# Picked attention of a graph and feed-forward network: two heads' scores laid behind each other in five banks, two banks for turned probabilities, contexts in one piece

## The reference, cut to what matters

```python
q = (normed @ Wq + bq).reshape(b, l, H, dh)      # H = 12 heads of dh = 64
kk = (normed @ Wk + bk).reshape(b, l, H, dh)
v = (normed @ Wv + bv).reshape(b, l, H, dh)
logits = jnp.einsum('blhd,bmhd->bhlm', q, kk) / jnp.sqrt(jnp.float32(dh))
probs = jax.nn.softmax(logits, axis=-1)
ctx = jnp.einsum('bhlm,bmhd->blhd', probs, v).reshape(b, l, d)
attn_out = ctx @ Wo + bo
merged = jnp.where(attn_mask[..., None], attn_out, mix_out)
```

## Time and profile before

| | us |
|---|---|
| median of 3 runs | 2976.41 |
| lowest, highest | 2974.64, 2977.48 |
| the profiled execution's own time | 2970.5 |
| its span | 2968.8 |
| attend_picked in it, first scores to last spread matmul | 2701.4 to 2870.7 |

### The profile page before, as it was taken

The page is one execution under the profiler, slowest core; times in us unless marked ns, Lnnn a source line. Parts: engine busy times, 40 slices in busy tenths (PEclk is TensorE's granted clock), DMA queues, the critical chain, the costliest instruction groups (busy, mean ns, idle before and its releaser), DMA issues. The chain is left out here.

```text
span 2968.8 us, 39008 instructions
## 1 busy us (share of the span) xinstructions
PE 2536.1 (85%) x14382; PEld 2118.7 (71%) x14383; DVE 2106.1 (71%) x3030; ACT 1315.0 (44%) x1649; POOL 310.4 (10%) x166
## 2 busy tenths in 40 slices
PE   6877894888856994799699999699999979998888
PEld 3556892232323994699699999599888769896668
DVE  6775899999974555699689988660567687136555
ACT  1573225989831000222578776221565563222431
POOL 0000000000003794000000000331000000000013
PEclk9997656999976997899899999899999999999989
DMA  2467542611104554455646643452634362311012
GB/s 69 131 174 180 150 150 67 237 52 35 35 33 178 189 197 158 154 180 160 201 121 181 170 118 90 150 171 81 187 122 129 102 194 70 85 54 59 1 41 80
DMA packets 174702, 366.47 MB, mean 123 GB/s; under 512 B 24871, under 2 KB 103541, under 8 KB 174034
## 3 DMA queue, kind: packets, MB, share of 16 engines
q1 hardware_dynamic: 122024, 274.54, 30.9%
q10 hardware_dynamic: 49312, 73.97, 7.4%
q0 software_dynamic: 3200, 15.73, 1.5%
HBM read 281.06 MB, written 83.12 MB: 123 GB/s over the span
## 5 line engine op out<-in xcount | busy, mean ns | idle before, releaser
L1649 PE MATMUL gat_acc<-far_u,gat_ft 125*65 125x512 f32 x720 | 286.3, 538 | 58.1 <-DVE far_u L1717 57.6
L2246 PE MATMUL rg_out<-rg_w,rg_hT 128*125 128x256 f32 (+1 forms) x900 | 276.6, 307 | 8.0 <-POOL rg_w L1185 8.0
L2247 PE MATMUL rg_out<-rg_w,rg_hT 128*125 128x256 f32 (+1 forms) x900 | 275.5, 306 | 0.0
L2248 PE MATMUL rg_out<-rg_w,rg_hT 128*125 128x256 f32 (+1 forms) x900 | 275.3, 306 | 0.0
L1649 PEld LDWEIGHTS gat_acc<-far_u,gat_ft 125*65 125x65 f32 x720 | 93.7, 142 | 246.9 <-issue 153.6
L2246 PE MATMUL rg2a_acc<-rg2a_value_part,rg2a_wts_part 125*125 125x512 f32 x600 | 204.8, 341 | 14.8 <-DVE rg2a_wts_part L1958 11.4
L2247 PE MATMUL rg2a_acc<-rg2a_value_part,rg2a_wts_part 125*125 125x512 f32 x600 | 205.5, 342 | 0.0
L2248 PE MATMUL rg2a_acc<-rg2a_value_part,rg2a_wts_part 125*125 125x512 f32 x600 | 203.8, 340 | 0.0
L1684 ACT ACTIVATE far_u<-gat_rows,gat_ks 125x1250 f32<-125x1250 f32 x118 | 156.7, 1328 | 41.8 <-PE gat_acc L1649 32.7
L2246 PEld LDWEIGHTS rg_out<-rg_w,rg_hT 128*125 128x125 f32 x900 | 169.1, 188 | 8.2 <-issue 8.0
L1697 DVE TENSOR_TENSOR far_u<-far_u,gat_lowb 125x1250 f32<-125x1250 f32 x120 | 174.4, 1454 | 0.4 <-PEq L711 0.4
(11 more groups left out here) (531 smaller groups left out, 6369.3 us busy)
## 6 DMA issues: line engine op xcount, KB each, us to landing
rg2a_values<-values_dram SPq DMA_DIRECT2D x89, 384.0 KB, 3.2
rg1a_counts<-counts_dram SPq DMA_DIRECT2D x26, 820.3 KB
rg_mask<-far_dram SPq DMA_DIRECT2D x60, 312.5 KB, 3.2
moe_raw<-in_L_ffn_w SPq DMA_DIRECT2D x16, 1152.0 KB, 6.9
relw_chunk<-in_L_gnn_W ACTq DMA_DIRECT2D x36, 384.0 KB, 3.1
gat_rows<-rows_dram SPq DMA_DIRECT2D x10, 1250.0 KB, 5.7
sorted_dram<-gat_zeros SPq DMA_DIRECT2D x30, 384.0 KB, 8.9
values_dram<-rg_stage ACTq DMA_DIRECT2D x90, 128.0 KB, 2.9
```

The source lines that it names most:

```text
L1649: last = pe.matmul(acc[h % 2][0:WIDTH, b, 0:c1 - c0], ft[:, t, h, :], wts[i % HB][:, c0:c1], start=(t == 0), stop=(t == NT - 1))
L2246: pe.matmul(out, still[0], moving[0], start=first, stop=False)
L2247: pe.matmul(out, still[0], moving[1], start=False, stop=False)
L2248: return pe.matmul(out, still[1], moving[0], start=False, stop=final)
```

## The change

All edits are in `attend_picked`.

- PSUM: the scores of a pair lie in one tensor of five banks, unit A in columns 0 to 1249, unit B in columns 1250 to 2499, so that the third bank holds the end of A and the start of B. The bank gained makes a second bank for turns: each half has its own. The context keeps its bank.
- The pieces of the scores are cut at the banks: A 226, 512, 512 columns and B 512, 452, 286, in this order A, B, A, B, A, B. Ahead of B's last piece, which lies in the shared bank, TensorE waits on a new semaphore `shared_made` for A's first piece, which lies there too.
- TensorE's order: both turns of unit i, then the context of unit i-1 in one piece. A turn waits for the copy of the same half of the unit before.
- VectorE: both first halves stand ahead of take_context(a-3).
- ScalarE: both copies of a unit stand ahead of both exponentials; an exponential waits for both first halves of its pair.
- `probs` has four buffers instead of three.

```diff
-    PB = 3
+    PB = 4
-        score_ps = [s.ps(f"att_score{i}", [128, 3, 512]) for i in range(2)]
-        turn_ps = s.ps("att_turn", [TP, 512])
+        all_ps = s.ps("att_score", [128, 5, 512])
+        score_ps = [all_ps[:, 0:2, :], all_ps[:, 2:4, :]]
+        turn_ps = [s.ps(f"att_turn{i}", [TP, 512]) for i in range(2)]
         ctx_ps = s.ps("att_ctx", [128, 512])
-        flat = [x[0:QT, :, :].rearrange("p a b -> p (a b)") for x in score_ps]
+        flat = [all_ps[0:QT, :, :].rearrange("p a b -> p (a b)")[:, i * N:(i + 1) * N] for i in range(2)]
+        pieces = [((1024, N), (1536 - N, 2048 - N)), ((0, 512), (2048 - N, N)), ((512, 1024), (0, 1536 - N))]
+        shared_made = s.sem("att_shared_made")
...
-                for k in range(0, N, 512):
-                    w = min(512, N - k)
-                    for i in (2 * p, 2 * p + 1):
+                for both in pieces:
+                    for i, (k0, k1) in zip((2 * p, 2 * p + 1), both):
                         q, h = units[i]
                         at = slice(h % 2 * DH, h % 2 * DH + DH)
-                        last = pe.matmul(flat[i % 2][:, k:k + w], qT[at, h // 2, q * QT:(q + 1) * QT],
-                                         kT[at, h // 2, k:k + w], start=True, stop=True)
+                        if i % 2 and k0 == 0:
+                            pe.wait_ge(shared_made, p + 1)
+                        last = pe.matmul(flat[i % 2][:, k0:k1], qT[at, h // 2, q * QT:(q + 1) * QT],
+                                         kT[at, h // 2, k0:k1], start=True, stop=True)
+                        if k1 == N and i % 2 == 0:
+                            last.then_inc(shared_made, 1)
                 last.then_inc(scored, 1)
 
             def turn(i, half):
                 if half == 0:
                     pe.wait_ge(scaled, i + 1)
-                if 2 * i + half:
-                    pe.wait_ge(turned_out, 2 * i + half)
+                if i:
+                    pe.wait_ge(turned_out, 2 * (i - 1) + half + 1)
...
-            def context(i, t0, t1):
+            def context(i):
...
             for i in range(len(units)):
                 if i % 2 == 0 and i + 2 < len(units):
                     scores(i // 2 + 1)
-                cut = 7 if i % 2 == 0 else NT
                 turn(i, 0)
+                turn(i, 1)
                 if i:
-                    context(i - 1, 0, cut)
-                turn(i, 1)
-                if i and cut < NT:
-                    context(i - 1, cut, NT)
+                    context(i - 1)
...
             for a in range(0, len(units), 2):
                 first_half(a)
+                first_half(a + 1)
                 if a >= 4:
                     take_context(a - 3)
-                first_half(a + 1)
                 second_half(a)
                 second_half(a + 1)
...
             def exponential(i):
-                act.wait_ge(topped, i + 1)
+                act.wait_ge(topped, i // 2 * 2 + 2)
...
-                    if i % 2 == 0 and i + 2 < len(units):
-                        exponential(i + 2 + half)
+                if i % 2 == 0 and i + 2 < len(units):
+                    exponential(i + 2)
+                    exponential(i + 3)
```

More of the change, by code:

```diff
@@ L3371, in turn @@
                     pe.wait_ge(scaled, i + 1)
-                if 2 * i + half:
-                    pe.wait_ge(turned_out, 2 * i + half)
+                if i:
+                    pe.wait_ge(turned_out, 2 * (i - 1) + half + 1)
                 for k in range(5):
                     t = half * 5 + k
-                    last = pe.transpose(turn_ps[:, k * QT:(k + 1) * QT], probs[i % PB][:, t * TP:(t + 1) * TP],
+                    last = pe.transpose(turn_ps[half][:, k * QT:(k + 1) * QT], probs[i % PB][:, t * TP:(t + 1) * TP],
                                         g.ident[0:QT, 0:QT])
                 last.then_inc(turned, 1)
-            def context(i, t0, t1):
+            def context(i):
                 q, h = units[i]
                 at = slice(h % 2 * DH, h % 2 * DH + DH)
[L3384 to L3388, removed]
+                pe.wait_ge(turned_out, 2 * i + 2)
+                if i:
+                    pe.wait_ge(ctx_out, i)
+                for t in range(NT):
                     last = pe.matmul(ctx_ps[at, 0:QT], v[:, t, h * DH:(h + 1) * DH],
                                      probsT[i % 2][:, t, :], start=(t == 0), stop=(t == NT - 1))
-                if t1 == NT:
-                    last.then_inc(ctx_made, 1)
+                last.then_inc(ctx_made, 1)
             def bias(q):
@@ L3413, in _ @@
             bias(0)
-            context(len(units) - 1, 0, NT)
+            context(len(units) - 1)
             bias(1)
@@ L3442, in first_half @@
                 dve.wait_ge(scored, i // 2 + 1)
-                link(dve.tensor_reduce(out=top[:, i:i + 1], in_=flat[i % 2][:, 0:N], op=ALU.max, axis=AX_X))
+                link(dve.tensor_reduce(out=top[:, i:i + 1], in_=flat[i % 2], op=ALU.max, axis=AX_X))
                 dve.tensor_scalar(top[:, i:i + 1], top[:, i:i + 1], -SCALE, None, op0=ALU.mult).then_inc(topped, 1)
@@ L3489, in exponential @@
             def exponential(i):
-                act.wait_ge(topped, i + 1)
+                act.wait_ge(topped, i // 2 * 2 + 2)
                 if i >= PB:
                     act.wait_ge(turned, 2 * (i - PB + 1))
-                act.activation(probs[i % PB][:, :], flat[i % 2][:, 0:N], ACT.Exp, bias=top[:, i:i + 1], scale=SCALE,
+                act.activation(probs[i % PB][:, :], flat[i % 2], ACT.Exp, bias=top[:, i:i + 1], scale=SCALE,
                                accum_out=total[:, i:i + 1]).then_inc(exp_done, 1)
@@ L3504, in _ @@
                     act.activation(probsT[i % 2][:, half * 5:half * 5 + 5, :].rearrange("p t q -> p (t q)"),
-                                   turn_ps[:, 0:5 * QT], ACT.Copy).then_inc(turned_out, 1)
-                    if i % 2 == 0 and i + 2 < len(units):
-                        exponential(i + 2 + half)
+                                   turn_ps[half][:, 0:5 * QT], ACT.Copy).then_inc(turned_out, 1)
+                if i % 2 == 0 and i + 2 < len(units):
+                    exponential(i + 2)
+                    exponential(i + 3)
             act.wait_ge(ctx_made, len(units))
```

## The result

| | median, us | runs | lowest, highest |
|---|---|---|---|
| before | 2976.94 | 4 | 2974.64, 2986.27 |
| changed | 2947.72 | 4 | 2943.46, 2950.96 |
| before, on the chip of the last experiments | 2975.75 | 11 | 2966.83, 2980.50 |
| changed, same chip | 2947.81 | 6 | 2942.43, 2953.61 |

The ratio is 0.9911, 95% interval 0.9891 to 0.9931, and on the other chip 0.9908 (0.9889 to 0.9926): 26.5 and 27.4 us, with intervals that reach from 20.5 to 33. The medians differ by 29.2 and 27.9 us. The profiled execution took 2943.46 us, its span 2941.7.

The account below looks back on a forecast made before the run. No engine is full; a chain through several sets the 10.35 us round, forecast to become 8.46. Start 0.4, nine rounds 17.0 and end 4.3 sum to 21.7 us off 2976.4: 2954.7 us, range 2950 to 2966.

Parts of the forecast that it names:

- Own work of TensorE: Attention round: scores, four turns and two contexts on TensorE take 8.37 us; 8.65 if turn-to-turn passages are not free.
- Chain beside it: Attention round through VectorE and ScalarE: scores, maxima, exponentials, next scores take 8.46 us, setting the round; ends 8.36 and 8.55.
- Pieces of unequal length: Scores on TensorE: unequal neighbouring pieces cost 0, scores stay 2.27 us; 0.48 us more if each neighbour waits for the longer.
- lockstep rival: Scores' pieces run in lockstep: scores 2.75 us, chain 8.94, TensorE 8.79; gain 15.9 us, 2960.5 us; chance 0.17.
- Shared bank's wait: Scores on TensorE: waiting for A's first piece ahead of B's last one costs nothing.
- fourth buffer: Probabilities' buffers: with three or four, no exponential waits for turns; effect 0.
- First rounds: Start of the stage: second scores 1.4 us later, third scores 0.4 us earlier; ends 1.7 earlier and 1.5 later.
- End: Last scores to output matmuls: 24.06 us now, gain 4.3 us; 2.6 with the clock's dip kept.
- the clock's dip: Last scores to output matmuls: the dip, mean clock 0.93 before, goes, since no gap above 0.7 us is left.
- Longer chain: Rival: exponential chain 1.0 us longer, round 9.46; gain 11.4 us, 2965 us; chance 0.11.
- no gain: Rival: copies of unit i+1 behind two exponentials bring the turns' wait back elsewhere; 2975.4 us; chance 0.06.
- slower clock: Rival: longer idle at the start keeps TensorE at 1.2 GHz; 3027 us if for all nine rounds; chance 0.04.

Follow-up runs that it names:

- the undone order: Changed kernel with TensorE's old order: context of odd units cut in 7 and 3 steps between the turns; rounds of 8.81 us, stage 118.48, whole 2956.27 us.
- the first trace: First profiled execution of the changed kernel, nothing further edited: 2943.46 us, stage 113.51 us; the changed kernel's repeated run had a stage of 115.03 us.

## Why the prediction was right, and where its sizes were off

The direction, the places and the size held: forecast 21.7 us less, 24.5 and 22.9 in the stage, 26.5 and 27.4 by the ratios. The range is met only at its edge: its lower end 2950 lies 2.3 us above the median 2947.72. The ratio, put on the forecast's base of 2976.4, gives 2949.9, and its interval of 2944 to 2956 holds the forecast 2954.7.

- *Own work of TensorE*, forecast 8.37: it is 8.34, with two turns at 1.26 (forecast 1.28). That the passage between two turns is free, which I took from another stage's matmuls, held; the undone order gives 0.16 for each passage. The Trainium skill's rule that a change of tiling mode drains TensorE ("TensorEngine Tiling (Array Packing)", Key Properties) agrees in direction; the size is from these rows.
- *Chain beside it*, forecast 8.46: 8.34. The mis-sized term is the distance of two exponentials, 1.29 and not 1.40. The accumulator's read does not hold the next exponential up: it starts at 2774.52 and takes 0.19 us, the exponential starts at 2774.61. Nine rounds by 0.12 are 1.1 us.
- *Pieces of unequal length*: scores still take 2.27 to 2.28 us. The lockstep rival (2.75) is out; the two halves of the array run on by themselves. In the round shown a record of A's second piece starts at 2768.17, while a record of B's first, 512 columns from 2767.72 on, runs until 2768.38 by the profile. The Trainium skill's rule that matmuls start and end in program order ("TensorE: Matmul & The Clock Gate", Part 3, The mechanism), taken strictly, does not fit these starts and ends; the measurement decides. (That rival's sum for TensorE is 8.37 + 0.48 = 8.85, not 8.79; its price rests on the chain's 8.94 all the same.)
- *Shared bank's wait, fourth buffer*: nothing, as forecast. For the buffer a run shows it, for the wait only that scores and round keep their length.
- *First rounds*, forecast 0.4 gained: 1.9 in one trace, 0.3 in the other. The second scores come 1.3 us later (8.40 instead of 7.12; forecast 1.4) when the first ones run at full clock, and 10.01 behind the first when they do not. Two steps were wrong. I kept the low clock until about 2721; it lasted 6.8 us in the first trace (from 2704.70) against 13.7 before. In the other it was low for 3.4 us from 2703.27 and for 6.8 from 2710.10. The first of these began 0.6 us behind the first scores, ahead of the long gap, so it is not that gap's doing. And I let TensorE's own work set the second round, where the exponentials set it (the wait of 1.47 us above). Why the low clock ended earlier is open: the round behind the gap has fewer gaps, but all runs with the new banks and an unfilled gap have the 6.8 there, the one with the old orders too.
- *End*, forecast 4.3: 4.5, and the clock's dip is gone. Of the foreseen waits for copies one is there (0.48).
- *Longer chain, no gain, slower clock*: all out. But the mechanism of the last is real: with all orders undone the clock fell once in every settled round.

The sum is thus 1.2 to 2.8 us short of the stage's gain, 1.1 of it the exponentials' distance. What the medians show beyond the stage's 24.5 I cannot assign.

## What to carry to other kernels

Read which instruction stands ahead of the late one in its own engine's queue: here a 0.32 us copy out of PSUM with a 1.7 us wait ahead of a ready reduction, and copies behind exponentials, held three engines that all had room. Such orders are worth changing together: any single one undone gives back between a quarter (0.47 of 2.01 us a round) and nearly all of it. The new orders with one turn bank, and the new banks with the old orders, were both slower than the kernel before. What one order alone would give in the kernel before was not run. When the round is gone down to one engine's full work, check by shortening each chain alone whether a second one lies level with it; if so, the next edit has to shorten both.

## What the runs showed of the hardware that I had not expected

- Matmuls on the upper and lower 64 rows with pieces of 226/512, 512/452 and 512/286 columns take 2.28 us together, as three equal pairs do.
- An exponential with its sum starts 1.29 us behind the one before (length 1.29), while the first one's accumulator read is still to end.
- Which gaps of TensorE were followed by a fall of the clock: 3.24 us in each round, in every settled round; 0.65 and 1.81, five times in nine rounds; 1.42, once in nine. A single 1.76 in rounds of 10.16, or 0.37 and 1.07 in the old rounds, had none in nine rounds. So the length of the longest gap alone does not sort them. The first low stretch behind the stage's start lasted 13.7 us before. In the new order it was 6.8 in five traces, and in three more 3.4, begun ahead of the long gap, and 6.8 from within it on, with full clock between.
- What such a low stretch costs depends on where it falls: one of 3.4 us cost a round 1.6 us with one turn bank, and the 6.8 us at the start of the changed kernel cost its second round 2.13.
